# A mixture-of-experts transformer block: value waves in groups, and three pieces of side work moved to the other ring of PSUM banks

## The chip, the cores and the metric

One core of a Trainium2 chip. Five engines run their own instruction streams and meet only at semaphores: TensorE (PE in the profile, its weight loads PEld), VectorE (DVE), ScalarE (ACT), GpSimd (POOL) and SyncE (SP). Matmul results go to PSUM, which has 8 banks of 512 fp32 columns on 128 partitions. The metric is the device time of one execution in microseconds (us), the median of several.

## The reference

`x` is 2048 tokens of 256 features, the context 1601 tokens. Cut to what matters:

```python
# attention over the context: 8 heads of 4 features, 2048 queries, 1601 keys
q, k, v = split_heads(layernorm(x) @ Wq + bq), split_heads(ctx @ Wk + bk), split_heads(ctx @ Wv + bv)
x = x + tanh(g_xattn) * (merge_heads(softmax(q @ k.T * scale) @ v) @ Wo + bo)
# feed-forward: 8 experts, each takes the 512 tokens with its highest router score
xn = layernorm(x)
scores = softmax(xn @ router_w + router_b)
G, idx = top_k(scores.T, 512)
h = relu(xn[idx] @ w1 + b1)
y = zeros.at[idx].add((h @ w2 + b2) * G)
x = x + tanh(g_ffn) * y
```

## The kernel before

Three stages follow one another: projections of the context (to 47 us), attention (47 to 342 us), and router, search for the best tokens and experts (to the end). The change touches attention only, and one wait of GpSimd beside it.

**Units and steps.** Queries are cut into 4 chunks of 512 (`NC`), each chunk into 4 units: 2 groups of 4 heads times 2 halves of 256 queries. So there are 16 units (`UNITS`), `u` from 0 to 15, and `r` is the unit's number in its chunk. A unit runs over 13 steps (`NKT`), `kt` from 0 to 12, of 128 keys. I write (r, kt) for a step of every chunk.

**The softmax without a maximum pass of its own.** Each row's maximum is found beforehand by bf16 matmuls of 802 scores ("max tiles", 16 of them for a unit, `max_tile` L1448), which VectorE reduces straight from PSUM (`mquart`, L1025). After a unit's sixteenth tile VectorE makes the negated maxima (`mparts`, L1037 to L1041), TensorE places them into the query operand (`place_max` L1466, at step `PLACE` of the unit before), and ScalarE copies this to `qfull`. `tiles_by` spreads the tiles so that they run about one unit ahead, 16 per 26 half steps.

**One step.** TensorE computes the scores of 4 heads in two halves (`scores` L1478, each fills one bank). ScalarE takes the exponential of each half (`exp`, L752) into `probs`, a ring of 6 steps. TensorE multiplies `probs` by the values of an earlier step: a "value wave" (`pv` L1488) is 4 matmuls on 32 columns of the array each, into bank 7. The profile counts 8, since fp32 goes in two passes. After the last wave ScalarE copies bank 7 to `osb` (`take_o`).

**Two rings of banks.** Banks 0 to 2 are ScalarE's ring: `next_act` hands them out in turn and makes TensorE wait until ScalarE has read what stood there three handings before. So the second half of the scores of a step waits for the first exponential of the step before. Banks 3 to 6 are VectorE's ring of two slots of two banks each: `next_dve` waits for the reader of two handings before. All engines work strictly in the order of their programs, which is written out by hand: at step `kt` TensorE issues tiles, both halves of scores, tiles, one value wave, and then what side work stands at this step.

**Side work of a chunk** is placed by constants: `O_THIS`, `O_LAST` (turn `osb`, VectorE normalises), `BACK_AT` (turn back), `WO_AT` (`wo` L1518, the output projection, ScalarE scales it, L773, and GpSimd adds it to `xs`, L504), `XN_AT` (turns of the first norm `xn`, L1387), `Q_AT` (projection of the next chunk's queries, L1393, then GpSimd splits them), `X2_AT` (turns of the second norm `x2`, L1529), `ROUTER_AT`, and `LN1_AT`, `LN2_AT` (statistics of both norms on VectorE).

**GpSimd** applies the norms, splits the queries, and, after the last full chunk, prepares the first expert's weights (`first_weights` L553): four pairs of two casts (L558, L560) and two subtractions (L562, L565).

Of the kernel before, what the change touches and what calls it, by code (L numbers as in the profile page):

```python
# [19 lines left out]
D = 256  # L20
# [88 lines left out]
def build(nc, x, ctxt, g_x, g_f, Wq, bq, Wk, bk, Wv, bv, Wo, bo, rw, rb, w1, b1, w2, b2, cf, cdigits, out, x2d):  # L109
# [9 lines left out]
    with es:  # L119
# [216 lines left out]
        def dve_bank(n):  # L336

            return 3 + 2 * (n % 2)
# [25 lines left out]
        LN1_AT = {(u, NKT - CT + t): (c, t) for c, u in ((2, 1), (3, PER_CHUNK + 1)) for t in range(CT)}  # L364
        LN2_AT = ((1, 4), (1, 5), (1, 6), (1, 7))
# [95 lines left out]
        def _(pool):  # L461
# [37 lines left out]
            def add_wo(c):  # L499

                pool.wait_ge(s_xb, c + 1)
                pool.wait_ge(s_wt, 2 * (c + 1))
                rows = xs[:, CT * c:CT * c + CT, :]
                nc.gpsimd.tensor_tensor(rows, rows, x2[:, :, :], ALU.add).then_inc(s_x1, 1)  # L504
# [48 lines left out]
            def first_weights():  # L553

                for pair in range(PAIRS):
                    a, f = 2 * P * pair, 2 * pair
                    pool.wait_ge(s_w1in[pair // 2], 16)
                    nc.gpsimd.tensor_copy(w1h[:, :, a:a + 2 * P], w1raw[:, :, a:a + 2 * P]).then_inc(s_w1h, 1)  # L558
                    pool.wait_ge(s_w2in[pair // 2], 16)
                    nc.gpsimd.tensor_copy(w2h[:, f:f + 2, :], w2raw[:, f:f + 2, :]).then_inc(s_w2h, 1)  # L560
                    pool.wait_ge(s_w1h, pair + 1)
                    nc.gpsimd.tensor_tensor(w1l[:, :, a:a + 2 * P], w1raw[:, :, a:a + 2 * P],  # L562
                                            w1h[:, :, a:a + 2 * P].bitcast(F32), ALU.subtract).then_inc(s_w1l, 1)
                    pool.wait_ge(s_w2h, pair + 1)
                    nc.gpsimd.tensor_tensor(w2l[:, f:f + 2, :], w2raw[:, f:f + 2, :],  # L565
                                            w2h[:, f:f + 2, :].bitcast(F32), ALU.subtract).then_inc(s_w2l, 1)
# [82 lines left out]
        def _(act):  # L649
# [118 lines left out]
            def scale_wo(c, odd, bank):  # L768
# [4 lines left out]
                nc.scalar.activation(x2[:, odd:CT:2, :], ps[:, bank, :].rearrange("p (t d) -> p t d", d=D), ACT.Copy,  # L773
                                     scale=tg[:, 0:1]).then_inc(s_wt, 1)
# [8 lines left out]
            def take_X(c, k, bank):  # L783

                act.wait_ge(s_X, KD * c + k + 1)
                take(x2T[:, k, :], ps[:, bank, :], s_Xt)
# [16 lines left out]
            def take_xn(c, k, bank):  # L803

                act.wait_ge(s_T, KD * c + k + 1)
                take(xnT[:, k, :], ps[:, bank, :], s_Tt)

            q_full(0)
            for u in range(UNITS):
                c, g, h, r = unit(u)  # L810
                for kt in range(NKT):
                    exp(u, kt, 0)
                    exp(u, kt, 1)
                    if kt == 1 and u > 0:
                        take_o(u - 1)
# [4 lines left out]
                    if c > 0 and (r, kt) == WO_AT:  # L820
                        for odd in range(2):
                            scale_wo(c - 1, odd, next_bank())
                    if c + 1 < NC and (r, kt) in XN_AT:
                        take_xn(c + 1, XN_AT.index((r, kt)), next_bank())
# [4 lines left out]
                    if c > 0 and (r, kt) in X2_AT:  # L829
                        take_X(c - 1, X2_AT.index((r, kt)), next_bank())  # L830
# [59 lines left out]
        def _(dve):  # L890
# [220 lines left out]
            for u in range(UNITS):  # L1111
                c, g, h, r = unit(u)
                for kt in range(NKT):
# [8 lines left out]
                    if c > 0 and (r, kt) in LN2_AT:  # L1122
                        ln2_stats(c - 1, LN2_AT.index((r, kt)))
                    if c > 0 and (r, kt - 1) == LN2_AT[-1]:
                        ln2_aggr(c - 1)
                    if (u, kt) in LN1_AT:
                        ln1_stats(*LN1_AT[u, kt])
                    if kt == 0 and (u - 1, NKT - 1) in LN1_AT:
                        ln1_aggr(LN1_AT[u - 1, NKT - 1][0])
# [218 lines left out]
        def _(pe):  # L1348
# [242 lines left out]
            for u in range(UNITS):  # L1591
# [4 lines left out]
                for kt in range(NKT):  # L1596
# [22 lines left out]
                    if c + 1 < NC and (r, kt) in XN_AT:  # L1619
                        k = XN_AT.index((r, kt))  # L1620
                        transpose_xn(c + 1, k, next_act((s_Tt, KD * (c + 1) + k + 1)))
# [3 lines left out]
                    if c > 0 and (r, kt) in X2_AT:  # L1625
                        k = X2_AT.index((r, kt))
                        transpose_x2(c - 1, k, next_act((s_Xt, KD * (c - 1) + k + 1)))
# [161 lines left out]
```

## Time and profile before

| | us |
|---|---|
| median of 3 runs | 592.31 (591.82 to 592.48) |
| the profiled execution | 591.86 |
| its span, first to last instruction | 590.1 |
| attention, from the copy to `qfull` of unit 0 to the last value wave | 47.4 to 342.0 |
| TensorE busy from 47.4 to 342.5 | 279.2 |
| VectorE busy there | 250.3 |
| ScalarE busy there | 247.7 |
| GpSimd busy there | 102.6 |

Lengths of stages are read from the span. A busy time is the sum of instruction lengths of an engine with overlaps counted once. A busy TensorE need not be at its peak, since matmuls are pipelined and their ends modelled: what a piece of TensorE's work costs is best read from the start of its first instruction to the start of the next one. In the timeline the brackets tell how long an engine was idle before a group and what ended that.

### The profile page before, as it was taken

The numbers are of one execution on the slowest core, as the hardware profiler recorded it, in microseconds if no ns is written. First come the engines' busy times: TensorE is split into PE (matmuls) and PEld (weight loads), VectorE is DVE, ScalarE is ACT, GpSimd is POOL, SyncE is SP. The second block draws the span as 40 slices with busy tenths as digits, with TensorE's granted clock in tenths as the row PEclk, the third lists the DMA queues.
The fourth block names the chain that finished last, engine by engine and source line by source line (L and its number), as shares of the span: only waits on it lengthen the run. The fifth ranks groups of instructions, "written<-read, shape, count | busy, mean of one in ns | idle before, by whom it ended". The sixth has DMA issues, their size and how long they took to land.

```text
span 590.1 us, 12821 instructions
## 1 busy us (share of the span) xinstructions
PE 549.7 (93%) x5043; PEld 318.8 (54%) x5043; DVE 446.4 (76%) x811; ACT 391.0 (66%) x762; POOL 214.4 (36%) x205
## 2 busy tenths in 40 slices
PE   7798899999999999999998988899999999999994
PEld 4433333334343333433333344479889898898973
DVE  3889879996999969899896268656767868676541
ACT  2587778987789878898887830054665656555651
POOL 3058075001925018200167010240644626446234
PEclk9999999999999999999999999999999999999998
DMA  8600000001000000100000105012735656355133
GB/s 280 244 2 1 1 1 3 2 1 38 2 37 2 2 37 1 38 1 2 37 37 2 38 18 163 18 55 81 167 110 108 153 134 144 107 109 160 19 37 36
DMA packets 23808, 35.80 MB, mean 61 GB/s; under 512 B 3460, under 2 KB 16197, under 8 KB 23621
## 3 DMA queue, kind: packets, MB, share of 16 engines
q1 hardware_dynamic: 17604, 26.59, 13.9%
q0 software_dynamic: 6144, 8.39, 8.1%
q8 instruction: 40, 0.66, 0.5%
q14 instruction: 20, 0.16, 0.1%
HBM read 26.59 MB, written 8.39 MB: 59 GB/s over the span
## 4 chain that ended last, share of the span: by engine, by line
PE 72%; DVE 17%; issue 4%; ACT 3%; POOL 1%; DMA 1%; POOLq 0%; DVEq 0%; ACTq 0%; SPq 0%
PE ps L1728 15%; PE ps L1735 15%; PE ps L1497 14%; DVE mquart L1025 9%; PE ps L1463 7%; PE ps L1484 7%; PE ps L1393 2%; PE ps L1354 2%; ACT probs L752 2%; PE ps L1369 1%; PE ps L1706 1%; PE ps L1681 1%; DVE mparts L1041 1%; PE ps L1506 1%; ACT osb L651 1%
## 5 line engine op out<-in xcount | busy, mean ns | idle before, releaser
L1025 DVE TENSOR_REDUCE mquart<-ps 128x2 f32<-128x802 f32 x256 | 240.6, 986 | 28.4 <-PE ps L1463 25.9
L752 ACT ACTIVATE probs<-ps 128x512 f32<-128x512 f32 (+1 forms) x416 | 223.6, 596 | 27.0 <-PE ps L1484 22.6
L1497 PE MATMUL ps<-probs,vp 128*32 128x256 f32 (+1 forms) x1664 | 133.5, 393 | 4.2 <-ACT osb L651 4.1
L1463 PE MATMUL ps<-kpad,qrows 64*128 64x401 bf16 x512 | 89.6, 337 | 5.9 <-DVE mquart L1025 5.0
L1484 PE MATMUL ps<-qfull,kpad 64*128 64x256 bf16 (+1 forms) x832 | 86.8, 273 | 1.1 <-ACT x L773 0.9
L1322 DVE TENSOR_TENSOR h1l<-hf,h1h 128x512 fp32r<-128x512 f32 x64 | 44.3, 692 | 55.8 <-ACT hf L877 45.9
L876 ACT ACTIVATE h1h<-ps,b1T 128x512 fp32r<-128x512 f32 x64 | 43.9, 687 | 54.3 <-PE ps L1728 52.5
L1735 PE MATMUL ps<-w2h,h1h 128*128 128x256 f32 x256 | 73.8, 288 | 2.2 <-DVE h1l L1322 1.5
L1735 PE MATMUL ps<-w2l,h1h 128*128 128x256 f32 x256 | 72.4, 283 | 0.0
L1735 PE MATMUL ps<-w2h,h1l 128*128 128x256 f32 x256 | 72.3, 282 | 0.0
L621 POOL DMA_INDIRECT out<-eo,idx_put x32 | 55.4, 1732 | 26.1 <-ACT eo L886 16.9
L1463 PEld LDWEIGHTS ps<-kpad,qrows 64*128 64x128 bf16 x512 | 25.9, 93 | 67.3 <-DVE mquart L1025 37.2
L1484 PEld LDWEIGHTS ps<-qfull,kpad 64*128 64x128 bf16 (+1 forms) x832 | 38.6, 96 | 43.4 <-ACT probs L752 21.7
L1497 PEld LDWEIGHTS ps<-probs,vp 128*32 128x32 f32 (+1 forms) x1664 | 33.3, 108 | 51.6 <-ACT probs L752 32.2
L1735 PEld LDWEIGHTS ps<-w2h,h1h 128*128 128x128 f32 x256 | 48.8, 191 | 6.6 <-issue 4.7
L1728 PE MATMUL ps<-tokh,w1h 128*128 128x512 f32 x128 | 51.0, 398 | 0.0
L1728 PE MATMUL ps<-tokh,w1l 128*128 128x512 f32 x128 | 50.4, 394 | 0.0
L1728 PE MATMUL ps<-tokl,w1h 128*128 128x512 f32 x128 | 50.0, 390 | 0.0
L1735 PEld LDWEIGHTS ps<-w2l,h1h 128*128 128x128 f32 x256 | 48.9, 191 | 1.3
L1735 PEld LDWEIGHTS ps<-w2h,h1l 128*128 128x128 f32 x256 | 48.9, 191 | 0.0
L599 POOL DMA_INDIRECT toks<-x_rows,idx_get x32 | 32.0, 1001 | 36.0 <-DVE idx_get L1300 24.9
L504 POOL TENSOR_TENSOR xs<-xs,x 128x1024 f32<-128x1024 f32 x3 | 7.1, 2354 | 101.4 <-ACT x L773 101.4
(200 smaller groups left out, 732.5 us busy)
## 6 DMA issues: line engine op xcount, KB each, us to landing
w1raw<-in_L_ffn_w SPq DMA_DIRECT2D x16, 512.0 KB, 4.7
w2raw<-in_L_ffn_w SPq DMA_DIRECT2D x16, 512.0 KB
xs<-in_x SPq DMA_DIRECT2D x4, 512.0 KB, 7.8
ctx_sb<-in_ctx SPq DMA_DIRECT2D x3, 512.0 KB, 6.0
out<-xs SPq DMA_DIRECT2D x3, 512.0 KB, 4.3
x_rows<-x SPq DMA_DIRECT2D x3, 512.0 KB, 2.6
b2b<-in_L_ffn_b SPq DMA_DIRECT2D x1, 1024.0 KB, 11.6
out<-xs SPq DMA_DIRECT2D x2, 256.0 KB, 2.0
```

Of the source, the lines that this page charges most:

```text
L599: nc.gpsimd.indirect_dma_start(out=toks[:, t, :], out_offset=None, in_=x2d, in_offset=bass.IndirectOffsetOnAxis(ap=idx_get[:, t:t + 1], ax ...
L621: nc.gpsimd.indirect_dma_start(out=out_rows, out_offset=bass.IndirectOffsetOnAxis(ap=idx_put[:, t:t + 1], axis=0), in_=eo[:, t, :], in_off ...
L752: nc.scalar.activation(out_p, ps[0:w, next_bank(), :], ACT.Exp, scale=float(SCALE)).then_inc(s_ex, 1)
L876: nc.scalar.activation(h1h[:, f, :], ps[:, bank, :], ACT.Relu, bias=bias).then_inc(s_hh, 1)
L1025: nc.vector.tensor_reduce(mquart[:, u % 2, t, a, :, kq], ps[:, b:b + 2, 0:MAXW], AX.X, ALU.max).then_inc(s_mr, 1)
L1322: nc.vector.tensor_tensor(h1l[:, f, :], hf[:, f % 2, :], h1h[:, f, :].bitcast(F32), ALU.subtract).then_inc(s_hl, 1)
L1354: mm(ps[:, SPARE, :].rearrange("p (r c) -> p r c", c=P), ident_bf[:, :], ident_bf[:, :].unsqueeze(1).to_broadcast([P, 4, P]), start=True, ...
L1463: last = mm(ps[:, bank + b, 0:MAXW], qrows[band(b), g, q:q + P], kpad[band(b), g, a, lo:lo + MAXW], start=True, stop=True)
L1484: last = mm(ps[0:w, bank, UW * b:UW * b + UW], kpad[band(p), g, b, P * kt:P * kt + w], qfull[band(p), g, UW * h:UW * h + UW], start=True, ...
L1497: last = mm(ps[32 * hh:32 * hh + 32, PV, 0:UW], vp[0:w, kt, g, hh, :], probs[0:w, step % PROBS, hh, :], start=(kt == 0), stop=(kt == NKT - 1))
L1728: last = mm(ps[:, UP_BANKS[f % 3], :], w[:, k, P * f:P * f + P], r[:, k, :], start=(m == 0), stop=(m == len(terms) - 1))
L1735: last = mm(ps[:, bank, a:a + D], h[:, f, P * t:P * t + P], w[:, f, :], start=(f == 0 and m == 0 and a == 0), stop=(f == NF - 1 and m == 2 ...
```

## The change

It moves work between engines' queues and between the two rings; no arithmetic changes.

- **Value waves** no longer follow every step. In units 0 to 14 they stand at steps 1, 4, 6, 8, 10 and 12, in groups of 2, 3, 2, 2, 2, 2 (`PV_GROUPS`); the group at step 1 is that of steps 11 and 12 of the unit before. Unit 15 keeps one wave a step. `osb` is copied after step 2's exponentials in place of step 1's.
- **Output projection and the turns of both norms** take one slot of VectorE's ring (two banks) in place of two banks of ScalarE's ring. ScalarE still reads them, with one instruction over 1024 columns in place of two over 512. VectorE's program only counts the slot. Both turns of a norm are issued in one go.
- **Positions:** the placing of maxima goes from step 10 to 11, `O_THIS` and `O_LAST` from 4 to 5, the projection from (0, 12) to (0, 9), the first norm's turns from (0, 9) and (0, 11) to (0, 9) for chunk 1 and (0, 3) later, the second query projection from (1, 6) to (1, 7), the second norm's turns from (2, 6) and (2, 7) to (2, 9), the router's from (2, 9) and (2, 12) to (2, 10) and (3, 0). Statistics: first norm, four tiles at steps 9 to 12 become two at step 7 and two at 8; second norm, four at steps 4 to 7 become two at 3 and two at 4.
- **GpSimd** waits before the third of the four weight pairs until the maxima of unit 15 are made (`s_mp` at `UNITS`).

```diff
-        PLACE = 10
-        O_THIS, O_LAST, BACK_AT, WO_AT = (2, 4), (0, 4), (0, 7), (0, 12)
-        XN_AT, Q_AT = ((0, 9), (0, 11)), ((1, 3), (1, 6))
-        X2_AT, ROUTER_AT = ((2, 6), (2, 7)), ((2, 9), (2, 12))
+        PLACE = 11
+        O_THIS, O_LAST, BACK_AT, WO_AT = (2, 5), (0, 5), (0, 7), (0, 9)
+        XN_FIRST, XN_LATER, Q_AT = (0, 9), (0, 3), ((1, 3), (1, 7))
+        X2_AT, ROUTER_AT = (2, 9), ((2, 10), (3, 0))
...
+        LN1_AT = {(u, kt): (c, ts) for c, u in ((2, 1), (3, PER_CHUNK + 1)) for kt, ts in ((7, (0, 1)), (8, (2, 3)))}
+        LN1_DONE = {(1, 9): 2, (PER_CHUNK + 1, 9): 3}
+        LN2_AT = {3: (0, 1), 4: (2, 3)}
...
+        PV_GROUPS = {1: (-2, -1), 4: (0, 1, 2), 6: (3, 4), 8: (5, 6), 10: (7, 8), 12: (9, 10)}
+
+        def values_at(u, kt):
+
+            ks = PV_GROUPS.get(kt, ()) if u < UNITS - 1 else (kt - 2,)
+            return [(u, k) if k >= 0 else (u - 1, NKT + k) for k in ks if u > 0 or k >= 0]
...
+        def take_at(u):
+
+            return 2 if u < UNITS - 1 else 1
...
                 for pair in range(PAIRS):
                     a, f = 2 * P * pair, 2 * pair
+                    if pair == PAIRS // 2:
+                        pool.wait_ge(s_mp, UNITS)
...
-            def take_xn(c, k, bank):
-
-                act.wait_ge(s_T, KD * c + k + 1)
-                take(xnT[:, k, :], ps[:, bank, :], s_Tt)
+            def take_xn(c, bank):
+
+                act.wait_ge(s_T, KD * (c + 1))
+                nc.scalar.activation(xnT[:, :, :], ps[:, bank:bank + KD, :], ACT.Copy).then_inc(s_Tt, KD)
...
+                    for name in dve_slots(u, kt):
+                        if name in ("wo", "xn", "x2"):
+                            next_bank()
...
-                    if kt > 1:
-                        pv(u, kt - 2)
-                    elif u > 0:
-                        pv(u - 1, NKT - 2 + kt)
+                    for step in values_at(u, kt):
+                        pv(*step)
...
-                        even = next_act((s_wt, 2 * (c - 1) + 1))
-                        wo(c - 1, range(CT), (even, next_act((s_wt, 2 * c))))
+                        even = next_dve((s_wt, c))
+                        wo(c - 1, range(CT), (even, even + 1))
...
-                        transpose_xn(c + 1, k, next_act((s_Tt, KD * (c + 1) + k + 1)))
+                        first = next_dve((s_Tt, KD * (c + 2)))
+                        for k in range(KD):
+                            transpose_xn(c + 1, k, first + k)
```

**TensorE in unit 3, a unit with no side work, steps 4 to 6.** `ps<-qfull,kpad` are scores, `ps<-kpad,qrows` max tiles, `ps<-probs,vp` value waves (4 matmuls each). Before:

```order
L1463 MATMUL ps<-kpad,qrows 128x401 x2
L1484 MATMUL ps<-qfull,kpad 128x256 x4
L1463 MATMUL ps<-kpad,qrows 128x401 x2
L1497 MATMUL ps<-probs,vp 32x256 x4
L1484 MATMUL ps<-qfull,kpad 128x256 x4
L1463 MATMUL ps<-kpad,qrows 128x401 x2
L1497 MATMUL ps<-probs,vp 32x256 x4
L1484 MATMUL ps<-qfull,kpad 128x256 x4
L1463 MATMUL ps<-kpad,qrows 128x401 x2
L1497 MATMUL ps<-probs,vp 32x256 x4
```

After, from the tile ahead of step 4's scores to the tile ahead of step 7's (line numbers are those of the new file):

```order
L1499 MATMUL ps<-kpad,qrows 128x401 x2
L1520 MATMUL ps<-qfull,kpad 128x256 x4
L1499 MATMUL ps<-kpad,qrows 128x401 x2
L1533 MATMUL ps<-probs,vp 32x256 x12
L1520 MATMUL ps<-qfull,kpad 128x256 x4
L1499 MATMUL ps<-kpad,qrows 128x401 x2
L1520 MATMUL ps<-qfull,kpad 128x256 x4
L1499 MATMUL ps<-kpad,qrows 128x401 x2
L1533 MATMUL ps<-probs,vp 32x256 x8
L1499 MATMUL ps<-kpad,qrows 128x401 x2
```

The three single waves become a group of three behind step 4 and a group of two behind step 6; step 5 has none, and so its scores and those of step 6 stand with only a tile between them.

**TensorE in unit 4, at the output projection** (`ps<-wo_sb,onT`). Before, at steps 11 and 12, with a turn of the first norm (`ps<-cst,xn`) close ahead:

```order
L1387 MATMUL ps<-cst,xn 128x128 x4
L1463 MATMUL ps<-kpad,qrows 128x401 x2
L1484 MATMUL ps<-qfull,kpad 65x256 x4
L1497 MATMUL ps<-probs,vp 32x256 x4
L1522 MATMUL ps<-wo_sb,onT 128x256 x4
L1463 MATMUL ps<-kpad,qrows 128x401 x2
L1484 MATMUL ps<-qfull,kpad 128x256 x4
L1463 MATMUL ps<-kpad,qrows 128x401 x2
L1497 MATMUL ps<-probs,vp 32x256 x4
L1484 MATMUL ps<-qfull,kpad 128x256 x4
```

After, at steps 9 and 10:

```order
L1520 MATMUL ps<-qfull,kpad 128x256 x4
L1499 MATMUL ps<-kpad,qrows 128x401 x2
L1558 MATMUL ps<-wo_sb,onT 128x256 x4
L1520 MATMUL ps<-qfull,kpad 128x256 x4
L1499 MATMUL ps<-kpad,qrows 128x401 x2
L1533 MATMUL ps<-probs,vp 32x256 x8
L1499 MATMUL ps<-kpad,qrows 128x401 x2
L1520 MATMUL ps<-qfull,kpad 128x256 x4
```

The projection now stands on a step without a wave, and the norm's turns are gone from here to step 3.

**ScalarE at the same place,** with the semaphores that each instruction waits for. Before:

```order
L752 ACTIVATE probs<-ps 128x512 [waits scores]
L651 ACTIVATE xnT<-ps 128x512 [waits xn_transposed]
L752 ACTIVATE probs<-ps 65x512 [waits pv_done,scores]
L752 ACTIVATE probs<-ps 65x512 [waits scores]
L773 ACTIVATE x<-ps,tg 128x2x256 [waits x2_stored,wo_done] x2
L752 ACTIVATE probs<-ps 128x512 [waits pv_done,scores]
L752 ACTIVATE probs<-ps 128x512 [waits scores]
L752 ACTIVATE probs<-ps 128x512 [waits pv_done,scores]
```

After, at steps 9 to 11:

```order
L782 ACTIVATE probs<-ps 128x512 [waits pv_done,scores]
L782 ACTIVATE probs<-ps 128x512 [waits scores]
L803 ACTIVATE x<-ps,tg 128x2x2x256 [waits x2_stored,wo_done]
L782 ACTIVATE probs<-ps 128x512 [waits pv_done,scores]
L782 ACTIVATE probs<-ps 128x512 [waits scores]
L782 ACTIVATE probs<-ps 128x512 [waits pv_done,scores]
```

The two scalings of 512 columns (`x` in these rows is `x2`) have become one of 1024, again behind a step's exponentials.

## Rows read from the trace of the kernel before

**Rows 1.** The page: busy time of each engine over the whole execution.
```profile
PE 549.7 (93%) x5043; PEld 318.8 (54%) x5043; DVE 446.4 (76%) x811; ACT 391.0 (66%) x762; POOL 214.4 (36%) x205
```

**Rows 2.** Windows from `qfull` to `qfull`: length; busy PE, PEld, DVE, ACT, POOL; clock.
```profile
64.20:84.90 20.70, 20.06 (x207) 7.53 (x205) 16.41 (x20) 16.03 (x31) 8.79 (x7) 1.00 0.01 2
...
102.60:118.00 15.40, 15.09 (x193) 5.46 (x191) 15.07 (x20) 14.48 (x28) 0.00 (x0) 1.00 0.01 2
118.00:135.20 17.20, 16.78 (x203) 6.58 (x204) 16.47 (x22) 15.27 (x32) 0.00 (x0) 1.00 0.01 2
135.20:157.00 21.80, 21.00 (x211) 8.23 (x208) 16.11 (x27) 17.21 (x34) 11.18 (x8) 1.00 0.07 25
...
300.40:321.00 20.60, 17.34 (x217) 7.25 (x219) 18.88 (x24) 15.81 (x32) 19.89 (x21) 1.00 0.07 27
```

**Rows 3.** Who waited for whom from 47 to 321 us: total, times, longest.
```profile
DVE mquart L1025 <- PE ps L1463: 23.4, 34, 2.0
...
PE ps L1497 <- ACT osb L651: 3.6, 12, 0.3
```

**Rows 4.** The timeline in unit 3: start, length, engine, line, tiles, [idle before].
```profile
107.40 0.39 ACT L651 ACTIVATE osb<-ps 128x256 f32<-128x256 f32 x1
107.67 1.10 ACT L752 ACTIVATE probs<-ps 128x512 f32<-128x512 f32 x2
...
108.69 0.38 PE L1484 MATMUL ps<-qfull,kpad 64*128 64x256 bf16 x4
...
109.00 0.64 PE L1497 MATMUL ps<-probs,vp 128*32 128x256 f32 x8
109.10 4.29 ACT L752 ACTIVATE probs<-ps 128x512 f32<-128x512 f32 x8 [0.33 <-PE ps L1484]
...
109.57 0.34 PE L1463 MATMUL ps<-kpad,qrows 64*128 64x401 bf16 x2
...
109.75 0.39 PE L1484 MATMUL ps<-qfull,kpad 64*128 64x256 bf16 x4
```

**Rows 5.** The timeline where a score matmul waits alone, unit 5, step 0.
```profile
140.10 0.28 PE L1484 MATMUL ps<-qfull,kpad 64*128 64x256 bf16 x1 [0.29 <-ACT x L773]
...
140.59 0.64 PE L1497 MATMUL ps<-probs,vp 128*32 128x256 f32 x8
```

**Rows 6.** The timeline after the last step: two value waves back to back.
```profile
340.95 1.07 PE L1497 MATMUL ps<-probs,vp 128*32 128x256 f32 x16
...
341.95 0.61 PE L1655 MATMUL ps<-rw_sb,cst 128*128 128x8 f32 x4
```

**Rows 7.** Groups by line: shapes, count; busy, mean ns; idle before, releaser.
```profile
L752 ACT ACTIVATE probs<-ps 128x512 f32<-128x512 f32 x384 | 206.7, 596 | 26.6 <-PE ps L1484 22.6
...
L651 ACT ACTIVATE xnT<-ps 128x512 f32<-128x512 f32 x8 | 4.7, 598 | 1.8 <-PE ps L1387 1.8
```

**Rows 8.** The timeline at two pieces of side work of chunk 1.
```profile
138.19 1.13 PE L1522 MATMUL ps<-wo_sb,onT 32*128 32x256 f32 x8 [0.20 <-ACT probs L752]
...
139.25 0.34 PE L1463 MATMUL ps<-kpad,qrows 64*128 64x401 bf16 x2
...
144.73 1.98 PE L1393 MATMUL ps<-xnT,wqr 128*128 128x512 f32 x4
...
146.64 0.34 PE L1463 MATMUL ps<-kpad,qrows 64*128 64x401 bf16 x2
```

**Rows 9.** The timeline at the end of unit 14: the last row maximum.
```profile
316.87 3.67 DVE L1041 TENSOR_TENSOR mparts<-nmax,mparts 128x8 bf16<-128x8 f32 x1
...
319.22 1.26 POOL L565 TENSOR_TENSOR w2l<-w2raw,w2h 128x512 fp32r<-128x512 f32 x1
...
320.60 0.28 PE L1472 MATMUL ps<-qrows,ident_bf 128*128 128x256 bf16 x1 [2.60 <-DVE mparts L1041]
```

**Rows 10.** The timeline just after it, in units 14 and 15.
```profile
321.88 0.75 PE L1484 MATMUL ps<-qfull,kpad 64*65 64x256 bf16 x4
...
325.36 0.40 PE L1484 MATMUL ps<-qfull,kpad 64*128 64x256 bf16 x4
```

More of the change, by code:

```diff
@@ L766, in q_full, with scale_wo @@
                 take(qfull[:, g, UW * h:UW * h + UW], ps[:, next_bank(), 0:UW], s_qf)
-            def scale_wo(c, odd, bank):
+            def scale_wo(c, bank):
                 act.wait_ge(s_W, c + 1)
@@ L772, in scale_wo @@
                 at_least(act, s_X, KD * c)
-                nc.scalar.activation(x2[:, odd:CT:2, :], ps[:, bank, :].rearrange("p (t d) -> p t d", d=D), ACT.Copy,
+                nc.scalar.activation(x2[:, :, :].rearrange("p (t o) d -> p o t d", o=2),
+                                     ps[:, bank:bank + 2, :].rearrange("p o (t d) -> p o t d", d=D), ACT.Copy,
                                      scale=tg[:, 0:1]).then_inc(s_wt, 1)
@@ L781, in take_N, with take_X @@
                 take(onT[:, a:b], ps[0:2 * NH * HD, bank, a:b], s_Nt)
-            def take_X(c, k, bank):
-                act.wait_ge(s_X, KD * c + k + 1)
-                take(x2T[:, k, :], ps[:, bank, :], s_Xt)
+            def take_X(c, bank):
+                act.wait_ge(s_X, KD * (c + 1))
+                nc.scalar.activation(x2T[:, :, :], ps[:, bank:bank + KD, :], ACT.Copy).then_inc(s_Xt, KD)
             def take_X_half(half, bank):
@@ L813, in _ @@
                     exp(u, kt, 1)
-                    if kt == 1 and u > 0:
+                    if kt == take_at(u) and u > 0:
                         take_o(u - 1)
@@ L820, in _ @@
                     if c > 0 and (r, kt) == WO_AT:
[L821 to L824, printed above, removed]
+                        scale_wo(c - 1, slot_bank(u, kt, "wo"))
+                    if c + 1 < NC and (r, kt) == xn_at(c):
+                        take_xn(c + 1, slot_bank(u, kt, "xn"))
                     if c + 1 < NC and (r, kt) in Q_AT:
@@ L1121, in _ @@
                         normalise(c - 1, 1, 0, next_bank())
[L1122 to L1124 removed]
+                    for name in dve_slots(u, kt):
+                        if name in ("wo", "xn", "x2"):
+                            next_bank()
+                    if c > 0 and r == 1:
+                        for t in LN2_AT.get(kt, ()):
+                            ln2_stats(c - 1, t)
+                    if c > 0 and (r, kt) == (1, 5):
                         ln2_aggr(c - 1)
                     if (u, kt) in LN1_AT:
[L1127 to L1129 removed]
+                        to, ts = LN1_AT[u, kt]
+                        for t in ts:
+                            ln1_stats(to, t)
+                    if (u, kt) in LN1_DONE:
+                        ln1_aggr(LN1_DONE[u, kt])
                     if (u, kt) == (UNITS - 1, 0):
@@ L1624, in _ @@
                         q_project(c + 1, k, next_act((s_xf, NKB + NG * (c + 1) + k + 1)))
-                    if c > 0 and (r, kt) in X2_AT:
-                        k = X2_AT.index((r, kt))
-                        transpose_x2(c - 1, k, next_act((s_Xt, KD * (c - 1) + k + 1)))
+                    if c > 0 and (r, kt) == X2_AT:
+                        first = next_dve((s_Xt, KD * c))
+                        for k in range(KD):
+                            transpose_x2(c - 1, k, first + k)
                     if c > 0 and (r, kt) == ROUTER_AT[0]:
```

21 lines of the change are left out of this document (14 added, 7 removed).

## The prediction, made before the changed kernel ran

> **What bounds the kernel now.** I read the page first, then attention unit by unit, then the timeline of one plain unit. On the page TensorE is busy 93% of the span [rows 1], which says where to look and not what a saving there is worth. In the window of unit 3, which has no side work, TensorE is busy 15.09 of 15.40 us, VectorE 15.07 and ScalarE 14.48 [rows 2]: three engines are level, and 16 tiles on VectorE set the pace. The units with side work take 17.2 to 21.8 us, with VectorE at 16.1 to 16.5: there it waits. Between 47 and 321 us VectorE is idle for TensorE 23.4 us in all [rows 3]. That is the most that a better order in attention can give back, beside one stall at its end (below). So the question is not how much TensorE time a grouped wave saves, but what the loop between TensorE and ScalarE does when TensorE stays away longer.
>
> **Part 1, the grouped waves: what TensorE saves.** A wave costs 0.57 us from its start to the next instruction's (109.00 to 109.57 [rows 4]). Two waves back to back take 1.00 (340.95 to 341.95 [rows 6]), so a joined wave costs 0.43 and saves 0.14 at its end, and perhaps as much again at its entry. 13 waves become 6 groups, 7 joints a unit: 1 to 2 us of TensorE's 15.
>
> The Trainium skill (TensorEngine Tiling (Array Packing), section Tiling Modes) says that changing the tiling mode drains the TensorE. Scores are on 64-row tiles and waves on 32-column tiles, and the saved 0.14 agrees. By this rule alone the change is a gain; that is my first rival.
>
> **Part 1, what the grouping costs.** ScalarE's ring has three banks, so the second half of a step's scores waits for the first exponential of the step before. The loop is made of four pieces. (a) From a second half of scores, issued alone, with a tile after it, to the wave: 0.49 (140.10 to 140.59 [rows 5]); without a tile some 0.16 less. (b) The group: 1.00. (c) From scores to their exponential: 0.41 (108.69 to 109.10 [rows 4]). (d) From the first exponential to the scores that need its bank: 0.65 (109.10 to 109.75 [rows 4]). Before, a wave of 0.57 follows each step, a+0.57 is 1.06, and c+d is 1.06 too, beside two exponentials in 1.08 (8 in 4.29 [rows 4]): TensorE's work of a step and ScalarE's round trip run beside each other. Now two steps go like this: second half of scores of an even step, group, scores of the odd step, first exponential, and only then the second half of the next even step. That is one chain, 0.49 + 1.00 + 0.41 + 0.65 = 2.55 us for two steps. VectorE needs 15.4 / 6.5 = 2.37 for them.
>
> For a whole unit: six groups, 15.30. The third wave of step 4's group, 0.43. At steps 0, 2, 7 and 11 a tile now stands between a group and the next scores, 0.18 each (109.57 to 109.75 [rows 4]), 0.72. No tile ahead of the group at step 12, -0.16. The placing of maxima at step 11 takes one bank of ScalarE's ring, so step 12's second half waits for one exponential more, 0.54. Between the groups at 1 and 4 lies one step more, whose two exponentials are in the chain, 1.08, with the copy of `osb`, 0.27 (107.40 to 107.67 [rows 4]). Sum 15.30 + 0.43 + 0.72 - 0.16 + 0.54 + 1.08 + 0.27 = 18.2 us, against 15.4 now. Bounds: 16.3 if ScalarE's ring never bound and only VectorE's two slots did (a tile must be issued within 1.3 us of the one before; the group of three exceeds it by 0.6, step 12's by 0.2), and 19 if each estimate is 2% to 5% short. I take 18.2, for every piece has a row. The wait on the `osb` copy (12 waits, 3.6 us [rows 3]) goes, since the next wave comes two steps later.
>
> **Part 2, side work on top of 18.2.** At an odd step TensorE idles some 0.75 us (1.06 less 0.31 for the scores), and the change puts most side work there. What does not fit: the query projection, 1.91 (144.73 to 146.64 [rows 8]), costs 1.4 at step 3 and 1.5 at step 7. The output projection, 1.06 (138.19 to 139.25 [rows 8]), 0.7; the second norm's turns, eight matmul pairs of 0.14 or 1.16, 0.8. The first norm's turns at (0, 3): the tile of step 4 must wait until ScalarE has done step 3's exponentials and then the copy of 1024 columns, and the group of three stands behind that tile, 1.3. The two turns of `osb` keep a slot until VectorE has reduced the tile before, 0.5 each. The turn back and the router's turn shift the three-bank ring by one exponential, 0.54 each. The router behind a group, 0.8. Chunks 1 and 2 have all of these: 8.6 us each. Chunk 0 has two projections and one turn, 3.4; chunk 3 up to unit 14 has 3.8. Together 24.4 us. These are estimates from the rows; I give the sum 8 us either way.
>
> One copy in place of two: a copy of 512 columns takes 598 ns [rows 7] and the next instruction starts 0.5 us after it, so 1024 in one go, some 1.0 us by the columns, gain at most 0.1. But TensorE's next use of that slot now waits for all of it.
>
> **Part 3, statistics** (8 a chunk) move beside the query projections, into VectorE's idle time. VectorE has some 2.7 us to spare in a unit of 18.2, so I cost this at nothing; if TensorE's loop were shorter, it would be worth 1 to 2 us a chunk. The earlier output projection gives GpSimd's addition 4 steps before the statistics; it needs 2.4 us, so nobody waits.
>
> **Part 4, GpSimd's wait.** At 316.87 VectorE's last small subtraction for the maxima of unit 15 takes 3.67 us and ends with GpSimd's last weight subtraction (319.22 + 1.26), and TensorE stands idle 2.60 us for it [rows 9]. Then TensorE is at half clock: from 321.88 to 325.36 two score steps, two waves and a turn take 3.48 us [rows 10], where 2 x (0.31 + 0.57) + 0.26 = 2.02 would do, 1.5 lost. The wait takes both away, 4.1 us. The second half of the weights then runs under unit 15, where VectorE is idle and nobody needs them for 25 us. The Trainium skill (SBUF — State Buffer, section SBUF: two separate sides) says that VectorE and GpSimd take a shared port pair as an exclusive lock when VectorE has two SBUF inputs. The trace agrees (3.67 us for 8 elements).
>
> **The sum.** From `qfull` of unit 1 to that of unit 15 (64.2 to 321.0) before: 256.8 us, the 2.6 of the stall in it. After: 14 x 18.2 + 24.4 = 279.2, so +22.4. Unit 0 is bound by VectorE (20 tiles); its group of three and the norm's slot cost 1 more. The clock gives back 1.5. Unit 15 and all behind it stay. +21.9: the span goes from 590.1 to 612.0. The profiled execution (591.86) and the median (592.31) differ by 0.45, so the median goes to 592.3 + 21.9 = **614 us**.
>
> **The rivals.** (A) *TensorE's saved time is given back.* If ScalarE has enough scores ahead, the loop above doesn't close, and shorter TensorE work plus side work on wave-free steps takes away half of VectorE's 23.4 idle us: -12 - 4.1, **576 us**. For it: TensorE busy 15.09 of 15.40, and 21.00 of 21.80 in unit 5's window [rows 2]. Against it: three banks hold one and a half steps, 1.6 us of exponentials, and half of one is spent when the group starts. It decides in the other direction if two steps take under 2.37. (B) *Only VectorE's two slots bind.* Units of 16.3: 14 x 16.3 + 24.4 = 252.6, -4.2, with +1 and -1.5, **588 us**. (C) *The change doesn't keep what it says of the slot or of the clock:* TensorE, busy some 75% of a unit of 18.2 (15.09 less 1.5), falls to half clock for stretches as after 320.6. Each 3.5 us stretch costs 1.5, so ten of them make **629 us**. Against it: in unit 14's window, busy 17.34 of 20.60 us, it was granted full clock [rows 2].
>
> **How the numbers follow.** 614 with its own range of 602 to 622: 0.68. Rival B and what lies between, 584 to 601: 0.10. Rival A, 572 to 583: 0.17. Above 622: 0.05. The range that holds 8 in 10 is 580 to 622: the first two and a part of A. A measurement of this kernel can tell about 0.2% from no change. Faster by over 0.2% are A and most of B, 0.25; within 0.2%, 0.02; slower, 0.73.
>
> **What would show it.** In the profile after: units without side work at 18 us and not 15.4; ScalarE's idle time before the exponentials, by far most of it ended by scores, at three times now's; gaps of 0.5 to 0.8 us on TensorE ended by exponentials, at the even steps; VectorE idle 2.7 us a unit. The last subtraction at 0.2 us and full clock after it show part 4. I am wrong if exponentials run on without a gap over a group, as they do over a single wave now, or if the unit stays below 16.

## The result, and the profile after

The changed kernel takes 611.62 us (median, 610.69 to 612.78), the kernel before 592.37 in the same comparison: 1.033 times the time, interval 1.031 to 1.035. The forecast was 614, with 580 to 622 as its range. It is slower by 19.2 us where 21.9 were worked out.

The profiled execution has a span of 610.5 us, 20.4 more than before. The page's first line, the answer to [rows 1]:

```profile
PE 557.9 (91%) x5043; PEld 338.6 (55%) x5043; DVE 444.1 (73%) x811; ACT 382.5 (63%) x753; POOL 215.1 (35%) x205
```

TensorE does the same 5043 matmuls in fewer changes of mode and is busy 8 us longer. That is not more work. A busy time is made of modelled ends, and I read the rise as matmuls that stand apart and so overlap less than matmuls in a row; no run separates this. In either case TensorE's busy time says nothing here of what the groups save, and a saving can stand beside a rise.

The windows from `qfull` to `qfull` of units 0, 1, 3, 4, 5 and 14, the answer to [rows 2] (columns as there: length; busy PE, PEld, DVE, ACT, POOL; clock):

```profile
48.45:68.85 20.40, 16.44 (x171) 7.08 (x170) 17.51 (x28) 13.81 (x26) 11.65 (x11) 0.92 0.00 1
68.85:90.36 21.51, 19.87 (x205) 8.40 (x202) 18.14 (x29) 15.39 (x32) 10.14 (x8) 1.00 0.01 2
...
108.85:126.99 18.14, 16.20 (x192) 7.15 (x191) 15.39 (x20) 13.90 (x30) 0.00 (x0) 1.00 0.01 1
126.99:147.65 20.66, 18.79 (x214) 8.87 (x213) 16.05 (x22) 16.16 (x33) 1.70 (x1) 1.00 0.01 2
147.65:168.60 20.95, 19.36 (x201) 8.28 (x199) 18.05 (x35) 15.25 (x31) 10.79 (x9) 1.00 0.07 27
...
323.99:343.00 19.01, 17.60 (x212) 8.11 (x211) 13.49 (x21) 15.19 (x31) 9.94 (x11) 1.00 0.08 30
```

Unit 3, without side work, takes 18.14 us; 15.40 before, 18.2 in the sum. All three busy engines now have idle time in it. No single engine is the bound, and that is the mark of a loop.

The timeline of unit 3 over two steps (weight loads and VectorE left out), the answer to [rows 4]:

```profile
118.61 0.28 PE L1520 MATMUL ps<-qfull,kpad 64*128 64x256 bf16 x1 [0.30 <-ACT probs L782]
...
119.10 1.07 PE L1533 MATMUL ps<-probs,vp 128*32 128x256 f32 x16
...
120.11 0.34 PE L1499 MATMUL ps<-kpad,qrows 64*128 64x401 bf16 x2
...
120.29 0.38 PE L1520 MATMUL ps<-qfull,kpad 64*128 64x256 bf16 x4
...
120.70 2.06 ACT L782 ACTIVATE probs<-ps 128x512 f32<-128x512 f32 x4 [0.68 <-PE ps L1520]
...
121.36 0.39 PE L1520 MATMUL ps<-qfull,kpad 64*128 64x256 bf16 x2 [0.30 <-ACT probs L782]
```

Read it as a circle. The second half of scores starts at 118.61, the group 0.49 later. The group holds TensorE for 1.01, a tile for 0.18. Then come the next scores, 0.41 until ScalarE starts on them, and 0.66 until the bank is free for the second half of scores that TensorE has been waiting to issue. Together 2.75 us for this pair of steps. ScalarE sits idle 0.68 in it for want of scores, and TensorE 0.30 for want of a bank.

The same in totals. First the groups by line and shape over the execution, the answer to [rows 7]; then who waited for whom in units 0 to 14 (48 to 343 us), the answer to [rows 3] (total, times, longest):

```profile
L782 ACT ACTIVATE probs<-ps 128x512 f32<-128x512 f32 x384 | 203.0, 604 | 66.5 <-PE ps L1520 66.5
```

```profile
ACT probs L782 <- PE ps L1520: 64.7, 87, 3.0
...
DVE mquart L1055 <- PE ps L1499: 44.3, 66, 1.9
...
PE ps L1520 <- ACT probs L782: 17.1, 60, 0.4
```

ScalarE's idle time ahead of its exponentials went from 26.6 to 66.5 us, and VectorE's wait for tiles from 23.4 to 44.3. The third wait, scores that wait for an exponential, is not in the list of the kernel before; there only their weight loads waited for one, 19.7 us. All of the 66.5 us are ended by scores and none by a value wave, so it is not the ring `probs` of 6 steps, whose places are given back in groups too, that holds ScalarE up.

Where the 20.4 us of the span came from:

| stretch | before | after | difference |
|---|---|---|---|
| up to `qfull` of unit 0 | 47.44 | 48.45 | +1.0 |
| unit 0 | 16.76 | 20.40 | +3.6 |
| units 1 to 14 | 256.83 | 274.15 | +17.3 |
| unit 15 and all behind it | 269.07 | 267.50 | -1.6 |

The first row is no effect of the change: in the profiles of kernels that are all alike up to there it lies anywhere from 47.0 to 48.7.

### The profile page after: what moved, and what is told of

It reads as the page before. It is cut to its first block, busy times and chain, and to the rows that moved or that the text cites. A ratio compares the mean times of both kernels' runs of the same rounds, so it can differ in the third digit from the quotient of the medians.

```text
span 610.5 us, 12810 instructions
## 1 busy us (share of the span) xinstructions
PE 557.9 (91%) x5043; PEld 338.6 (55%) x5043; DVE 444.1 (73%) x811; ACT 382.5 (63%) x753; POOL 215.1 (35%) x205
## 4 chain that ended last, share of the span: by engine, by line
PE 73%; DVE 10%; ACT 10%; issue 4%; POOL 1%; DMA 1%; POOLq 0%; ACTq 0%; DVEq 0%; SPq 0%
PE ps L1533 16%; PE ps L1764 15%; PE ps L1771 14%; PE ps L1520 9%; ACT probs L782 9%; PE ps L1499 7%; DVE mquart L1055 4%; PE ps L1429 2%; PE ps L1390 2%; PE ps L1405 1%; PE ps L1742 1%; PE ps L1717 1%; POOL out L651 1%; PE ps L1558 1%; DVE ge L1242 1%
## 5 line engine op out<-in xcount | busy, mean ns | idle before, releaser
L782 ACT ACTIVATE probs<-ps 128x512 f32<-128x512 f32 (+1 forms) x416 | 220.2, 604 | 66.6 <-PE ps L1520 66.5
L1520 PE MATMUL ps<-qfull,kpad 64*128 64x256 bf16 (+1 forms) x832 | 113.6, 273 | 19.4 <-ACT probs L782 17.1
L1533 PE MATMUL ps<-probs,vp 128*32 128x256 f32 (+1 forms) x1664 | 112.5, 389 | 0.3 <-ACT osb L681 0.3
L1499 PE MATMUL ps<-kpad,qrows 64*128 64x401 bf16 x512 | 94.6, 338 | 6.8 <-DVE mquart L1055 4.9
L1520 PEld LDWEIGHTS ps<-qfull,kpad 64*128 64x128 bf16 (+1 forms) x832 | 45.5, 96 | 75.5 <-ACT probs L782 54.4
L1358 DVE TENSOR_TENSOR h1l<-hf,h1h 128x512 fp32r<-128x512 f32 x64 | 44.3, 692 | 56.0 <-ACT hf L907 52.1
L1533 PEld LDWEIGHTS ps<-probs,vp 128*32 128x32 f32 (+1 forms) x1664 | 43.9, 110 | 42.2 <-ACT probs L782 12.6
L1499 PEld LDWEIGHTS ps<-kpad,qrows 64*128 64x128 bf16 x512 | 27.4, 93 | 57.7 <-issue 26.2
L1390 PE MATMUL ps<-ident_bf 128*128 128x512 bf16 x149 | 39.8, 400 | 4.2 <-ACT ident_bf L716 4.2
```

What stands on the lines that cost most here:

```text
L782: nc.scalar.activation(out_p, ps[0:w, next_bank(), :], ACT.Exp, scale=float(SCALE)).then_inc(s_ex, 1)
L1358: nc.vector.tensor_tensor(h1l[:, f, :], hf[:, f % 2, :], h1h[:, f, :].bitcast(F32), ALU.subtract).then_inc(s_hl, 1)
L1390: mm(ps[:, SPARE, :].rearrange("p (r c) -> p r c", c=P), ident_bf[:, :], ident_bf[:, :].unsqueeze(1).to_broadcast([P, 4, P]), start=True, ...
L1499: last = mm(ps[:, bank + b, 0:MAXW], qrows[band(b), g, q:q + P], kpad[band(b), g, a, lo:lo + MAXW], start=True, stop=True)
L1520: last = mm(ps[0:w, bank, UW * b:UW * b + UW], kpad[band(p), g, b, P * kt:P * kt + w], qfull[band(p), g, UW * h:UW * h + UW], start=True, ...
L1533: last = mm(ps[32 * hh:32 * hh + 32, PV, 0:UW], vp[0:w, kt, g, hh, :], probs[0:w, step % PROBS, hh, :], start=(kt == 0), stop=(kt == NKT - 1))
```

## The experiments

**One part alone, one part undone.** `b_groups` is the kernel before with grouped waves and nothing else:

```diff
-                    if kt > 1:
-                        pv(u, kt - 2)
-                    elif u > 0:
-                        pv(u - 1, NKT - 2 + kt)
+                    for step in values_at(u, kt):
+                        pv(*step)
...
-                    if kt == 1 and u > 0:
+                    if kt == (2 if u < UNITS - 1 else 1) and u > 0:
```

> The kernel before with the grouped waves as its only edit (and the copy of osb a step later, which they need); rings, positions and GpSimd stay. The loop theory (second half of scores, group, next scores, exponential, freed bank, 2.55 us for two steps): units without side work at 18.1 us and not 15.4, 14 x 2.8 = 39 us less what side work finds of idle time on TensorE, at most its 38.6 us above 15.4 a unit and by the changed kernel's measure some 18: 612 to 628. The rival that only VectorE's two slots bind: units of 16.3, 592 to 605. The rival that the groups save TensorE's time and the rest of the change costs it: 585 or less.

Measured: 616.78 us (616.26 to 617.1), 1.041 times the kernel before, inside the range of the loop theory. `a_single` is the changed kernel with its waves undone:

```diff
-            ks = PV_GROUPS.get(kt, ()) if u < UNITS - 1 else (kt - 2,)
+            ks = (kt - 2,)
...
-            return 2 if u < UNITS - 1 else 1
+            return 1
```

> The changed kernel with one value wave a step again and the osb copy after step 1; slots, positions, statistics and GpSimd's wait as changed. The loop theory: units without side work back at 15.4 to 15.8 us; GpSimd's wait -4.1 and the statistics beside the projections up to -3 against the kernel before: 585 to 588. The rival that the two-bank slots and the new positions carry a part of the loss: 595 or more.

Measured: 588.74 us (587.8 to 589.8), 0.7 us above the range given. The window of unit 3 in `b_groups`, then in `a_single`:

```profile
106.40:124.37 17.97, 15.89 (x193) 7.15 (x193) 15.39 (x19) 14.01 (x28) 0.00 (x0) 1.00 0.01 1
```

```profile
102.70:118.41 15.71, 15.26 (x193) 5.56 (x191) 15.24 (x20) 14.47 (x30) 0.00 (x0) 1.00 0.01 2
```

The groups alone bring the loss and taking them out removes it. In the changed kernel they cost 22.9 us (611.62 less 588.74). Slots, positions and GpSimd's wait together are worth 5 us where waves are grouped (616.78 against 611.62). Up to 1.9 us of that can be VectorE's last small subtraction for the maxima, which takes 2.10 us at 343.68 in `b_groups`, beside a weight subtraction of GpSimd, and 0.19 where the two do not meet (`a_nowait`, below). By units it is a difference of two larger terms: units 1 to 14 take 6.6 us less in the changed kernel (274.15 against 280.74), and unit 0 takes 2.0 more (20.40 against 18.38).

**GpSimd's wait, alone and undone.** `b_wait` is the kernel before with these two lines, `a_nowait` the changed kernel without them:

```diff
+                    if pair == PAIRS // 2:
+                        pool.wait_ge(s_mp, UNITS)
```

> The kernel before with GpSimd's wait as its only edit. My theory: the last small subtraction for the maxima of unit 15 takes 0.2 us in place of 3.67, TensorE's gap of 2.60 us goes, and so does the half clock behind it (1.5 us): -4.1, 588.2 us. Rival: GpSimd's second half of the weights then falls on the router and the search, where VectorE and GpSimd work together, and gives the time back: 592 us.

> The changed kernel without GpSimd's wait. If VectorE's last subtraction meets GpSimd's weight subtractions as in the kernel before: +2.6 for the gap and up to +1.5 for the clock, 614 to 616 us. If the later end of unit 14 has moved it away from them: 611.6 us, and the wait was worth nothing here.

Measured: `b_wait` 588.95 us (588.4 to 589.43), 0.8 above what was expected, and `a_nowait` 611.25 (610.42 to 612.18), as its second case had it. The last subtraction for the maxima in `b_wait`, and the window of its unit 14 (20.60 before):

```profile
317.21 0.20 DVE L1043 TENSOR_TENSOR mparts<-nmax,mparts 128x8 bf16<-128x8 f32 x1
```

```profile
300.73:318.71 17.98, 17.30 (x216) 7.28 (x217) 15.83 (x24) 15.83 (x33) 14.02 (x16) 1.00 0.08 31
```

The same place in `a_nowait`, GpSimd's last weight subtraction and VectorE's:

```profile
336.39 1.28 POOL L593 TENSOR_TENSOR w2l<-w2raw,w2h 128x512 fp32r<-128x512 f32 x1
...
339.30 0.19 DVE L1069 TENSOR_TENSOR mparts<-nmax,mparts 128x8 bf16<-128x8 f32 x1
```

In the kernel before the wait brings 3.4 us. Between the traces unit 14 is 2.7 us shorter and all behind it 1.2, while attention starts 0.3 later. In the changed kernel it brings nothing that can be told. The attention before it takes so much longer that GpSimd is done 1.6 us before VectorE comes to its subtraction. `a_single` and `b_wait` are level (588.74 and 588.95), so with single waves parts 2 and 3 come to nothing in sum. They are not without effect: unit 0 takes 1.3 us more in `a_single` and unit 4 2.6 more, units 2 and 5 1.3 and 1.2 less.

**Which term closes the loop.** Three runs change one term of the circle, or something beside it. `a_halfexp` shortens the first exponential of each step:

```diff
-                out_p = probs[0:w, step % PROBS, 2 * p:2 * p + 2, :].rearrange("p h q -> p (h q)")
-                nc.scalar.activation(out_p, ps[0:w, next_bank(), :], ACT.Exp, scale=float(SCALE)).then_inc(s_ex, 1)
+                heads = 2 if p == 1 or step < PROBS else 1
+                out_p = probs[0:w, step % PROBS, 2 * p:2 * p + heads, :].rearrange("p h q -> p (h q)")
+                nc.scalar.activation(out_p, ps[0:w, next_bank(), 0:UW * heads], ACT.Exp, scale=float(SCALE)).then_inc(s_ex, 1)
```

> The changed kernel with the first exponential of each step over 256 columns in place of 512 (two of its four heads are left out, after the first six steps of the program; the output is then not the reference's). It shortens one term of the loop alone: the freed bank comes 0.21 us sooner (596 ns for 512 columns, 384 to 392 ns for a copy of 256). The loop theory: a plain unit goes from 18.1 to 16.7 us, and the whole to 590 to 597 us. The rival that TensorE's own work sets the pace (busy 16.20 of 18.14 us): 610 us or more, since TensorE's program is the same.

Measured: 598.64 us (598.35 to 599.39). `a_halftile` halves what VectorE reads of a tile:

```diff
-                nc.vector.tensor_reduce(mquart[:, u % 2, t, a, :, kq], ps[:, b:b + 2, 0:MAXW], AX.X, ALU.max).then_inc(s_mr, 1)
+                nc.vector.tensor_reduce(mquart[:, u % 2, t, a, :, kq], ps[:, b:b + 2, 0:MAXW // 2], AX.X, ALU.max).then_inc(s_mr, 1)
```

> The changed kernel with VectorE reducing only half the columns of each tile (200 of each bank's 401, so the maxima are of half the keys and the output is not the reference's). Nothing of the loop between TensorE and ScalarE is touched. The loop theory: plain units stay at 17.9 to 18.2 us, the whole at 606 to 612 us. The rival that the two slots of VectorE's ring bind behind a group: a tile's 0.93 us becomes some 0.5, units fall below 17 us, and the whole to 597 or less.

Measured: 604.17 us (603.5 to 604.86), 1.8 below the range given. `a_ahead` changes the order on TensorE:

```diff
-                    scores(u, kt, 0)
+                    if (u, kt) not in ahead:
+                        scores(u, kt, 0)
                     scores(u, kt, 1)
...
+                    if u < UNITS - 1 and kt in PV_GROUPS and kt + 1 < NKT and (r, kt) != ROUTER_AT[0]:
+                        scores(u, kt + 1, 0)
+                        ahead.add((u, kt + 1))
                     for step in values_at(u, kt):
```

> The changed kernel with the first half of the next step's scores issued ahead of each group, so that ScalarE has one exponential more in hand while TensorE is at the group (not at step 12, nor at the router's step). If the three banks of the ring are what closes the loop, the same chain only starts half a step later: scores, group 0.32 + 1.00, second half 0 to 0.18, exponential 0.41, freed bank 0.65, so 2.38 to 2.55 us for two steps in place of 2.55 to 2.73: plain units at 16.8 to 18.1 us, the whole at 594 to 611 us. The rival that the order alone keeps scores from ScalarE: plain units at 15.4 to 16, the whole at 590 or less.

Measured: 611.08 us (610.53 to 612.95), at the upper end of its range. The windows of unit 3 in `a_halfexp`, `a_halftile` and `a_ahead`, in this order:

```profile
105.95:123.01 17.06, 16.51 (x192) 7.21 (x191) 15.21 (x21) 11.20 (x30) 0.00 (x0) 1.00 0.01 1
```

```profile
102.76:120.89 18.13, 16.08 (x192) 7.22 (x191) 9.41 (x20) 13.90 (x29) 0.00 (x0) 1.00 0.01 1
```

```profile
107.82:125.48 17.66, 16.02 (x191) 7.55 (x191) 15.06 (x20) 13.90 (x30) 0.00 (x0) 1.00 0.00 1
```

With 5.98 us less of VectorE's work the unit takes 18.13 us, where it took 18.14: VectorE's ring is not in the loop of a plain unit, and the rival that only its two slots bind falls. With ScalarE's first exponential shorter the unit loses 1.08 us although TensorE's program is the same: so ScalarE's half of the circle counts, and TensorE's own work does not set the pace. It lost less than the 1.4 worked out, and the whole came out 1.6 us above the range given. The distances from the start of one group to the next, in unit 3, show where:

| steps | 12 to 1 | 1 to 4 | 4 to 6 | 6 to 8 | 8 to 10 | 10 to 12 |
|---|---|---|---|---|---|---|
| changed kernel | 2.74 | 4.00 | 3.00 | 2.74 | 2.58 | 3.07 |
| `a_halftile` | 2.74 | 4.00 | 3.01 | 2.74 | 2.57 | 3.07 |
| `a_halfexp` | 2.72 | 3.61 | 2.80 | 2.71 | 2.36 | 2.86 |

Four distances lose 0.2 us or more, as the circle wants. Two hardly move, and the pair of steps laid out above is one of them (2.74 and 2.71): with its circle shortened, the weight load of TensorE's next tile waits 0.29 us for VectorE's reduction (at 118.01 in `a_halfexp`). So in this pair the way through VectorE's slots comes close behind the circle. Scores issued ahead of the group bring 0.5 us a plain unit and nothing that can be told in all. ScalarE has one half more in hand, but the three banks are then full and the same chain starts half a step later. So the order alone is not the fault. That the ring is too short for a group fits all of this; the direct test, a ring of four banks, was not made, so that is argued and not shown.

`a_halftile` fell 2 us below its range, and the place is not the loop of a plain unit. Its profile is 8.8 us shorter than the changed kernel's: 1.4 ahead of attention, 3.8 in unit 0, and 3.6 in units 1 to 14, all of it in units with side work (unit 6 takes 19.02 us and not 19.56). There VectorE's reductions do count. Its unit 0:

```profile
47.05:63.67 16.62, 15.27 (x173) 7.09 (x171) 10.95 (x28) 13.58 (x26) 12.11 (x11) 1.00 0.00 1
```

It takes 16.6 us at full clock in place of 20.4 at 0.92. That led to the next run.

**Unit 0 and the clock.** The changed kernel at the first group of three, TensorE's timeline, and two windows of it:

```profile
54.16 0.49 PE L1499 MATMUL ps<-kpad,qrows 64*128 64x401 bf16 x2 [0.16 <-DVE mquart L1055]
54.59 2.79 PE L1533 MATMUL ps<-probs,vp 128*32 128x256 f32 x24
57.31 0.49 PE L1499 MATMUL ps<-kpad,qrows 64*128 64x401 bf16 x2
```

```profile
49.11:54.16 5.05, 3.52 (x32) 1.35 (x26) 5.02 (x11) 4.24 (x9) 4.21 (x6) 1.00 0.01 3
54.16:57.31 3.15, 3.15 (x27) 1.09 (x28) 1.75 (x2) 0.87 (x2) 3.15 (x3) 0.51 0.00 0
```

The granted clock is 0.51 there, the lower of TensorE's two levels (1.2 GHz). The group takes 2.72 us to the next start. The same group in unit 3, at full clock, takes 1.43:

```profile
116.10 1.50 PE L1533 MATMUL ps<-probs,vp 128*32 128x256 f32 x24
...
117.53 0.40 PE L1520 MATMUL ps<-qfull,kpad 64*128 64x256 bf16 x4
```

Before the clock fell TensorE had been busy 3.52 of 5.05 us, with the first waves put off. The same stretch of the kernel before, with waves at steps 2 and 3, has it busy 4.19 of 5.01, and the clock stayed at 1.00:

```profile
48.10:53.11 5.01, 4.19 (x45) 1.45 (x40) 4.97 (x11) 4.13 (x8) 4.16 (x6) 1.00 0.01 3
```

`a_u0single` keeps single waves in unit 0:

```diff
-            ks = PV_GROUPS.get(kt, ()) if u < UNITS - 1 else (kt - 2,)
+            ks = PV_GROUPS.get(kt, ()) if 0 < u < UNITS - 1 else (kt - 2,)
```

> The changed kernel with single waves in unit 0 only; units 1 to 14 stay grouped. In the changed kernel unit 0 takes 20.4 us, with a stretch at half clock from 54.2 to 57.3; with single waves throughout it took 18.1 at full clock. If the group of three, which starves the engines early in attention, is what lets the clock fall: unit 0 at 18.1 us at clock 1.00, the rest unchanged, 609.3 us. If the clock falls whatever the waves do there, as it does for other work: unit 0 at 19.5 us or more, 611 us.

Measured: 609.47 us (608.8 to 609.68). Its unit 0:

```profile
48.44:66.51 18.07, 16.45 (x179) 6.34 (x179) 17.39 (x28) 13.96 (x27) 11.67 (x11) 1.00 0.01 2
```

The clock stays full and unit 0 gives back 2.3 us. Some 1.3 of it is the slow group itself (2.72 less 1.43); the other 1.0 lies behind it or belongs to the grouping as such, and no run separates these. Late waves alone do not bring the drop: in `a_halftile`, whose tiles come sooner, unit 0 is grouped too, TensorE was busy 4.57 of the 5.05 us ahead of the first group, the clock stayed at 1.00 and the group took 1.44. The other five traces with grouped waves in unit 0 all have the drop. Whether every execution has it is open: the other three of the changed kernel have a mean granted clock of 0.996, 0.989 and 0.996 and take 610.95, 612.78 and 610.69 us, and were not traced.

**Two attempts at a faster kernel.** `b_stats` is `b_wait` with the first norm's statistics where the change puts them; `s_firstxn` is `a_single` with the first norm's turns for chunk 1 in ScalarE's ring:

```diff
-        LN1_AT = {(u, NKT - CT + t): (c, t) for c, u in ((2, 1), (3, PER_CHUNK + 1)) for t in range(CT)}
+        LN1_AT = {(u, kt): (c, ts) for c, u in ((2, 1), (3, PER_CHUNK + 1)) for kt, ts in ((7, (0, 1)), (8, (2, 3)))}
```

> The kernel before with GpSimd's wait and with the first norm's statistics at steps 7 and 8 of units 1 and 5 (two tiles each), as the change has them; waves, rings and all other positions stay. In the kernel with single waves the two units after these took 1.3 and 1.5 us less than in the kernel before, and the units themselves 0.4 more or 1.2 less, but there other positions had moved too. If the statistics are the reason: 586 to 587 us, 2 to 3 us under the kernel with the wait alone. If VectorE's work is only shifted from one unit to another: 588.9 us.

```diff
-                                            ("wo", c > 0 and (r, kt) == WO_AT), ("xn", c + 1 < NC and (r, kt) == xn_at(c)),
+                                            ("wo", c > 0 and (r, kt) == WO_AT), ("xn", 0 < c and c + 1 < NC and (r, kt) == xn_at(c)),
...
+                    if c == 0 and (r, kt) in ((0, 9), (0, 11)):
+                        k = (kt - 9) // 2
+                        transpose_xn(1, k, next_act((s_Tt, KD + k + 1)))
```

> The kernel with single waves (slots, positions and GpSimd's wait as changed), and the first norm's turns for chunk 1 back in ScalarE's ring, one at step 9 and one at step 11 of unit 0, as in the kernel before. There unit 0 takes 16.8 us and with the slot 18.1, since TensorE's next tile waits 0.2 us and more for ScalarE's copy of 1024 columns while VectorE, with 20 tiles, sets the pace. Expected if the slot is the cost: unit 0 at 16.8 us, 587.4 us in all, under every kernel so far. If the new positions of the rest set unit 0's end: 588.7 us.

Measured: `b_stats` 589.24 us (589.13 to 590.08), `s_firstxn` 588.42 (588.18 to 589.3). Neither beats its base (588.95 and 588.74) by what can be told. In `b_stats` unit 2 takes 0.4 us less than in `b_wait` (17.20, 17.64) but unit 1 takes 0.4 more (21.09, 20.73), and unit 5 0.6 more: the statistics are only shifted. In `s_firstxn` unit 0 takes 17.09 us and not 18.07, so the slot was 1.0 of its cost, but unit 1 gives back half of it. `s_firstxn`, `a_single` and `b_wait` stand at 588.4 to 589.0 us and beat both the kernel before and the changed one; `b_wait` is the simplest of them, with two lines.

## Why the prediction was right, point by point

- **What bounds the kernel before.** Three level engines with almost no idle time in a plain unit, so that the question is the loop and not TensorE's saving. This held: the wait that was there for the taking (23.4 us of VectorE's) grew to 44.3.
- **The circle.** Its four pieces were put at 0.49, 1.00, 0.41 and 0.65, with 0.18 where a tile stands in it. In the trace after they are 0.49, 1.01, 0.41, 0.66 and 0.18. (The 2.55 of the prediction is without the tile, the 2.75 of this pair with it.) A plain unit was put at 18.2 and takes 18.14. `a_halftile` shows that VectorE's reductions are not in it, `a_halfexp` that the exponential is, by the four distances that shrink; for this pair the pieces are read from the trace.
- **What the group saves.** A third wave was put at 0.43; the group of three takes 1.43, so the figure holds. The trace also agrees with what the Trainium skill says of draining at a change of tiling mode (TensorEngine Tiling (Array Packing), section Tiling Modes): 1.43 for three waves, where three single ones take 1.71 (3 x 0.57). The saving is real and worth nothing here.
- **Side work** was put at 24.4 us above the plain units and comes to 20.2 (274.15 less 14 x 18.14). By the prediction's terms, added up for the units of chunk 1: unit 4 was put at 3.0 and costs 2.5, unit 5 2.9 and 2.8, unit 6 2.1 and 1.4, unit 7 0.5 and 0.5. Two places carry the excess. The output projection was put at 0.7: from the group ahead of it to the group behind it there are 3.06 us (142.02 to 145.08), where a plain pair takes 2.73, so it costs 0.3. That is unit 4's excess; the norm's turns at step 3, put at 1.3, cost 1.2 (unit 4 20.66, unit 12, which is like it but for them, 19.48). And a turn of `osb`, the second norm's turns and the router behind a group were put at 2.1 together and come to 1.4 in units 6 and 10 and to 0.9 in unit 14. Each was costed by itself; that they share one gap would explain it, but no run takes them apart.
- **Unit 0** was put at +1 and came to +3.6. For its size this is the term that was most off. The clock was looked at only over whole units, and the rival with the clock (C) was priced with stretches like the one after 320.6. One such stretch came, not ten, at a place that the prediction did not name: the first group, before which TensorE had been given less to do. With the grouping it cost 2.3 us by `a_u0single`, of which 1.3 is the slow group. The slot and the new positions are the other 1.3 (18.07 less 16.76), and they alone use up the 1 us given for slot and group together. The sign was in the change itself: the first wave moves back by two steps, in a unit that VectorE sets the pace of.
- **GpSimd's wait** was credited with 4.1 us. About that much is in the result (no stall in unit 14, 1.6 us less behind it), but the wait did not bring it: `a_nowait` is level, so this term came out right by luck. The mechanism was right for the kernel before, where it is worth 3.4. What failed is the step that took a collision of two engines as fixed while both moved, and not alike: GpSimd's last subtraction starts 17.2 us later (336.39, before 319.22) and VectorE's small one 22.4 later (339.30, before 316.87).
- **Statistics at nothing:** no run has them alone beside grouped waves. `b_stats` has the first norm's beside single waves, where the loop is shorter and the prediction gave all statistics 1 to 2 us a chunk, and finds nothing. For this half of them that remark was wrong.
- **The rivals.** A (TensorE's time is given back, 576) and B (only VectorE's slots bind, 588) are both out by unit 3's window and by `a_halftile`. The errors in size are -4.2 for side work, -0.8 for the plain units, -0.1 behind them, +2.6 for unit 0 and +1.0 for the start. They take the 21.9 of the sum to the 20.4 of the span. Errors of 5.1 us down and 3.6 up mostly cancel, so the closeness of the total is in part luck. That of the plain units, 14 x 2.8 us forecast and 14 x 2.7 measured, is not.

What the prediction expected of the rows held, with two sizes off. ScalarE's idle time is 2.5 times what it was, not three times. TensorE's gaps are 0.2 to 0.4 us and not 0.5 to 0.8, because idle time is counted from the modelled end of a matmul: 0.28 us after its start, where an unhindered one is followed by the next within half of that. It would have been better to name distances between starts.

Open: how the 5 us that slots, positions and GpSimd's wait bring with grouped waves divide among them, what a fourth bank in ScalarE's ring would do, and what grouped waves in unit 0 cost at full clock.

## What to carry to other kernels

Before work is gathered on one engine to save its entry costs, look at how many buffers the engine behind it has: write down the circle from one use of a buffer to its next, with the gathered work in it, and compare it with the pace now (2.37 us for two steps before). Here three banks cover 1.6 us of exponentials, and a group of 1.00 us makes a circle of 2.55 to 2.75, and the kernel loses 22.9 us where 0.14 us a joint is saved. And a collision between two engines is a matter of when: credit its removal only if the rest of the change leaves the meeting where it is.

## What the runs showed of the hardware

- The granted clock fell to half behind a stretch in which TensorE was less busy than at the same place of the kernel before (3.52 of 5.05 us against 4.19 of 5.01; 4.18 of 5.00 in `a_u0single`, where it did not fall either). With grouped waves and TensorE busy 4.57 of 5.05 us (`a_halftile`) it did not fall. In no grouped unit after the first did it fall either, with TensorE busy 16.20 of 18.14 us in unit 3. A change that delays the first work of a kind can so cost more than the delay, if the work that comes then is long: 1.3 us on one group of 24 matmuls.
- One copy of 1024 columns on ScalarE takes 1056 ns (its group by line follows). One of 512 took 598, and the next instruction started 0.5 us after it (133.75 and 134.24 before), so two in a row are an estimated 1.1. As costed, joining them gains nothing to speak of.

```profile
L837 ACT ACTIVATE xnT<-ps 128x1024 f32<-128x1024 f32 x3 | 3.2, 1056 | 0.9 <-PE ps L1423 0.9
```

- VectorE's subtraction of 8 elements a partition in [rows 9] lasted as long as GpSimd had work, not for one instruction of it. It starts at 316.87. GpSimd's last two casts and two subtractions start at 316.87, 317.43, 318.00 and 319.22 without a gap, and it ends at 320.54, 0.06 us after the last of them. In `b_wait`, with GpSimd held back, it takes 0.20.
